# Graph attention, second layer: all row gathers issued in one run, outputs kept in gathered rows, dot products and sums alternating by tile

## The chip, the cores and the metric

The kernel runs on one core of one Trainium2 chip. The metric is device time in microseconds (us) of that core, median of three executions. One further execution was recorded by the profiler; every row below comes from it, and its times count from the start of its span.

## The reference

Two residual layers over N = 2048 nodes with D = 512 features; `adj` is a sparse 0/1 matrix with at most 8 neighbours in a row for these inputs. All is float32.

```
h = relu(layernorm(x));  x = x + GAT(h, adj)        # first layer: 16 heads, leaky relu, softmax, elu
h = relu(layernorm(x));  x = x + dense_att(h, adj)  # second layer

second layer:  q, k, v = h @ Wq.T + bq, h @ Wk.T + bk, h @ Wv.T + bv
               z = (q @ k.T) / sqrt(D) * adj;  z = where(z == 0, -10000, z)
               x + relu(softmax(z) @ v)
```

A node needs the `h` rows of its few neighbours and, for the masked entries, the sum of all rows times one small weight. A node without neighbours gets the mean of all rows.

## The kernel before

Nodes are ranked by their number of neighbours and handled in T = 16 tiles of 128 nodes. `SLOTS` says how many neighbours a tile keeps: 1, 1, 1, 1, 0, 8, 2, 5, 2, 4, 2, 3, 2, 3, 2, 3, in all 40. One gather fetches one neighbour row (512 floats) for each of the 128 nodes of a tile, so the layer has 40 gathers. GpSimd issues them (`gather1`, L1188 to L1191) as indirect DMAs out of `h1_dram`, where the first layer has stored `h` tile by tile (L1185), and counts them in `got[t]`.

The second layer, by engine. Each engine works through its own list in the order written; semaphores link the lists.

- TensorE (PE): `queries(t)` (L1275, L1278) makes u = h (Wq, Wk), most of it while the first layer still runs; the last ones of that stretch are tiles 12 and 13, tiles 14 and 15 come inside the second layer (`U1_AT`). One matmul with ones sums all rows of `h` (L1305). Then per tile k `transposes1(k)` (L1318, called T(k) here) turns the weighted sum, and `products(k)` (L1329, L1331, called P(k)) multiplies it by Wv. The order is T(k), P(k-1), but P(k-1), T(k) where k opens a part.
- VectorE (DVE): `dot(t)` (L929) waits for all slots of the tile and takes one dot product of u with each gathered row. Over a part of several tiles (`PARTS`) `scores1` (L948 to L953) masks and finds the maximum, `normalise1` (L960 to L967) makes the weights, and `aggregate1(t)` (L973) adds weight times row into `hb[t % 4]`, one instruction a slot.
- ScalarE (ACT): copies u out of PSUM (`copy_u`, L1026 and L1027), takes the exponentials of a part (`exp_scores1`, L1083, L1084), fills `hb` with the weighted sum of all rows (`base_of`, L1076), copies the transposes to SBUF (L1104) and applies the last relu (`output`, L1091) into one of four buffers `o_t`.
- GpSimd (POOL): after `gather1` of tiles 0 to 8 (21 gathers) it alternates `put(t)` (L1195), an indirect DMA that adds the tile's output to `out` in DRAM, with `gather1(9 + t)`. The residual x1 was stored to `out` in the first layer (L1177) for every tile.

The DVE list before is: wait for the sum matmul, copy it (L982), `constants`, then dots, scores and weights of tiles 0 to 3 and their sums; then for each part all its dots and scores, with the sums of the part before (the last of them between scores and weights). The ACT list before begins with `copy_u(13)` and then `exp_scores1(0)`, `base_of(0)`, `base_of(1)`. In its loop over k it waits for T(k), copies it, runs `exp_scores1` if k + 2 opens a part, then `base_of(k + 2)`, then `output(k - 1)`, which waits for P(k-1).

`row(k)` places gathered row k in buffers that the first layer has done with: 20 in `shared`, the next in `x1`, the last four in `w_out`.

Of the kernel before, what the change touches and what calls it, by code (L numbers as in the profile page):

```python
# [6 lines left out]
ALU = mybir.AluOpType  # L7
ACT = mybir.ActivationFunctionType
# [47 lines left out]
U1_AT = {4: 14, 6: 15}  # L56
# [15 lines left out]
QK_AT = (4, 7, 10)  # L72
NBAD = TOP + 1 + 2 * T + T * TOP
# [540 lines left out]
def sparse_layers(nc, v):  # L614
# [8 lines left out]
    with ctx:  # L623
# [92 lines left out]
        out_stored = [sem(f"out_stored{i}") for i in range(4)]  # L716
# [6 lines left out]
        o_t = [lone[:, 0, :], lone[:, 1, :], lone[:, 2, :], bv_bc[:, :]]  # L723
# [4 lines left out]
        PARTS = [(0, 4), (5, 2), (7, 2), (9, 3), (12, 4)]  # L728
# [4 lines left out]
        def row(k):  # L733
            if k < FLAT_ROWS:
                return shared[:, k * D:(k + 1) * D]
            if k < FLAT_ROWS + T:
                return x1[:, k - FLAT_ROWS, :]
            return w_out[:, k - FLAT_ROWS - T, :]
# [10 lines left out]
        with block:  # L749
            @block.vector  # L750
            def _(dve):
# [188 lines left out]
                def scores1(g):  # L940
                    t0, n = PARTS[g]
                    zz, qq, m = z[:, t0:t0 + n, :], zq[:, t0:t0 + n, :], zm[:, t0:t0 + n]
                    for t in range(t0, t0 + n):
                        dot(t)
                    if t0 == EARLY:
                        constants(EARLY, T)
                    dve.wait_ge(dot_done, dots[0])
                    step(dve.tensor_tensor(zz, zz, zp[:, t0:t0 + n, :], ALU.add))  # L948
                    step(dve.tensor_scalar(qq, zz, 0.0, NONE, ALU.is_equal, ALU.mult))
                    step(dve.tensor_tensor(zz, zz, qq, ALU.add))  # L950
                    step(dve.tensor_reduce(m, zz, AX_X, ALU.max))
                    step(dve.tensor_scalar(m, m, NONE, None, ALU.max))
                    dve.tensor_tensor(zz, zz, bc(zm, t0, n), ALU.subtract).then_inc(z_ready, 1)  # L953
# [26 lines left out]
                step(dve.memset(z[:, :, :], 0.0))  # L980
                dve.wait_ge(h_sum_mm, 1)
                dve.tensor_copy(h_sum, bank[0]).then_inc(sums_ready, 1)  # L982
                constants(0, EARLY)
                scores1(0)
                normalise1(0)
                for t in range(4):
                    aggregate1(t)
                for g in range(1, len(PARTS)):
                    t0, n = PARTS[g]
                    if g > 1:  # L990
                        for t in range(PARTS[g - 1][0], t0 - 1):
                            aggregate1(t)
                    scores1(g)
                    if g > 1:
                        aggregate1(t0 - 1)
                    normalise1(g)
                for t in range(*(PARTS[-1][0], T)):
                    aggregate1(t)

            @block.scalar  # L1000
            def _(act):
# [68 lines left out]
                copy_u(13)  # L1070
# [9 lines left out]
                def exp_scores1(g):  # L1080
                    t0, n = PARTS[g]
                    act.wait_ge(z_ready, g + 1)
                    act.activation(z[:, t0:t0 + n, :], z[:, t0:t0 + n, :], ACT.Exp)  # L1083
                    act.activation(e0[:, t0:t0 + n], zm[:, t0:t0 + n], ACT.Exp, bias=none[:, :], scale=-1.0).then_inc(z_exp, 1)  # L1084
                    act.wait_ge(weights_ready, g + 1)

                def output(t):
                    act.wait_ge(o_done, t + 1)
                    if t >= 4:
                        act.wait_ge(out_stored[t % 4], 16 * (t // 4))  # L1090
                    act.activation(o_t[t % 4], bank[2 + t % 4], ACT.Relu).then_inc(o_ready, 1)  # L1091

                act.wait_ge(sums_ready, 1)
# [3 lines left out]
                exp_scores1(0)  # L1097
                base_of(0)
                base_of(1)
                for k in range(T):  # L1100
# [4 lines left out]
                    if k + 2 < T:  # L1105
                        if k + 2 in first_of:
                            exp_scores1(first_of[k + 2])
                        base_of(k + 2)
                    if k >= 1:
                        output(k - 1)  # L1110
                    if k in U1_AT:
                        copy_u(U1_AT[k])
                output(T - 1)
# [10 lines left out]
            def _(pool):  # L1124
# [46 lines left out]
                for t in range(T):  # L1171
# [5 lines left out]
                    pool.indirect_dma_start(out[:, :], bass.IndirectOffsetOnAxis(own[:, t, :], 0), x1[:, t, :], None).then_inc(x1_stored, 16)  # L1177
# [15 lines left out]
                def put(t):  # L1193
                    pool.wait_ge(o_ready, t + 1)
                    pool.indirect_dma_start(out[:, :], bass.IndirectOffsetOnAxis(own[:, t, :], 0),  # L1195
                                            o_t[t % 4], None, compute_op=ALU.add).then_inc(out_stored[t % 4], 16)

                pool.wait_ge(hid_ready, T - 2)
                pool.wait_ge(x1_stored, T * 16)
# [3 lines left out]
                for t in range(9):  # L1203
                    gather1(t)
                for t in range(T):
                    put(t)
                    if 9 + t < T:
                        gather1(9 + t)
                for i in range(4):
                    pool.wait_ge(out_stored[i], T // 4 * 16)  # L1210

            @block.tensor
            def _(pe):
# [88 lines left out]
                queries(12)  # L1302
                pe.wait_ge(summed, T)
                pe.wait_ge(hidT_done, T)
                pe.matmul(bank[0], ones[:, 0:P], h_acc).then_inc(h_sum_mm, 1)  # L1305
                queries(13)
# [374 lines left out]
```

## Time and profile before

| | us |
|---|---|
| three executions | 498.70, 500.84, 495.36 |
| median | 498.7 |
| the profiled execution | 501.12 |
| its span | 499.6 |
| its mean granted TensorE clock | 0.912 of full |
| busy in the span: PE, DVE, POOL, ACT | 396.3, 371.2, 273.6, 244.4 |

The span runs from the first to the last instruction of the program; the time lies some 1.5 us above it. Busy shares are means over the whole program. The change touches the second layer alone, from about 360 us of the span on, so they say little here. The first layer's last tile is normalised at about 360 us, the last matmul of the program ends at about 481.5 us.

### The profile page before, as it was taken

To read this page: it belongs to the slowest core of one execution; us is meant where nothing else is said; L and a number is where in the kernel's file an instruction comes from. 1 tells how busy PE (TensorE), PEld (TensorE's weight loads), DVE (VectorE), ACT (ScalarE), POOL (GpSimd) and SP (SyncE) were. 2 spreads that over 40 slices of the span, in tenths; PEclk is the share of its full clock that TensorE was granted. 3 is DMA by queue.
4 is the path that set the end of the run, shared out by engine and by line. 5 is a ranking of instruction groups with operands and counts; after the bars stand their busy time and mean duration, and the time that the engine had idled before them with its cause. 6 is when DMAs were issued, how large, how long until landed. Compare 5 with 4: busy or idle time off the path is not lost.

```text
span 499.6 us, 6189 instructions
## 1 busy us (share of the span) xinstructions
PE 396.3 (79%) x2033; PEld 287.0 (57%) x2044; DVE 371.2 (74%) x715; ACT 244.4 (49%) x511; POOL 273.6 (55%) x283
## 2 busy tenths in 40 slices
PE   2899999994979888886778698889890499896950
PEld 2788888783867777852546454555680255443520
DVE  2999999977899898958679898778511478987300
ACT  1579777848888697823222344353510342342310
POOL 1344422236886776866705877774567268861330
PEclk9699999997999898999797988999997599997995
DMA  7979997300002432354413344531246347863450
GB/s 268 409 292 363 362 354 288 127 31 3 8 7 27 125 88 87 91 167 150 133 61 103 111 128 147 171 131 62 106 152 209 102 105 150 168 143 46 62 64 3
DMA packets 24290, 70.00 MB, mean 140 GB/s; under 512 B 6208, under 2 KB 6464, under 8 KB 22080
## 3 DMA queue, kind: packets, MB, share of 16 engines
q0 software_dynamic: 14336, 42.63, 31.0%
q1 hardware_dynamic: 9536, 26.96, 14.7%
q8 instruction: 17, 0.28, 0.2%
q14 instruction: 17, 0.14, 0.1%
q10 hardware_dynamic: 384, 0.00, 0.0%
HBM read 52.45 MB, written 17.12 MB: 139 GB/s over the span
## 4 chain that ended last, share of the span: by engine, by line
DVE 28%; PE 17%; POOL 15%; issue 10%; DMA 4%; ACT 1%; SPq 0%; DVEq 0%; ACTq 0%
PE psum L1331 6%; POOL record_dram L1127 4%; PE psum L1278 3%; PE psum L1234 3%; POOL s_shared L1147 3%; POOL s_shared L1165 3%; POOL s_rs L1176 2%; DVE s_shared L835 2%; DVE w_seq L929 2%; DVE s_shared L769 2%; DMA s_shared<-seq_dram,tab 2%; DVE s_shared L762 2%; DVE s_shared L760 2%; DVE s_st L853 2%; DVE s_x L851 2%
## 5 line engine op out<-in xcount | busy, mean ns | idle before, releaser
L1008 ACT ACTIVATE s_shared<-psum,seq_all 128x320 bf16<-128x320 f32 x192 | 81.6, 584 | 15.2 <-PE psum L1234 11.1
L1234 PE MATMUL psum<-s_shared 128*128 128x198 bf16 x768 | 76.4, 261 | 8.6 <-POOL s_shared L1147 8.6
L1234 PEld LDWEIGHTS psum<-s_shared 128*128 128x128 bf16 x768 | 71.5, 101 | 14.6 <-POOL s_shared L1147 10.3
L532 PE MATMUL psum<-w_seq,hT 128*128 128x272 f32 x256 | 63.2, 402 | 0.0
L1256 PE MATMUL psum<-w_out,hT 128*128 128x512 f32 x128 | 60.7, 620 | 0.9 <-ACT hT L1042 0.5
L1278 PE MATMUL psum<-w_qk,s_early 128*128 128x257 f32 x240 | 57.4, 393 | 0.0
L532 PEld LDWEIGHTS psum<-w_seq,hT 128*128 128x128 f32 x256 | 48.9, 195 | 10.0 <-issue 0.3
L1278 PEld LDWEIGHTS psum<-w_qk,s_early 128*128 128x128 f32 x240 | 46.5, 199 | 7.0
L1054 ACT ACTIVATE h_t<-s_x,s_nm,s_rs 128x512 f32<-128x512 f32 x16 | 13.0, 814 | 64.6 <-DVE s_nm L864 64.6
L1165 POOL DMA_INDIRECT s_shared<-seq_dram,tab x28 | 34.9, 1246 | 10.8 <-issue 8.2
L456 DVE MAX8 near<-adj_ring 128x8 f32<-128x2048 f32 x16 | 36.5, 2284 | 5.7 <-DMA adj_ring<-in_adj_dram 5.7
L1256 PEld LDWEIGHTS psum<-w_out,hT 128*128 128x128 f32 x128 | 25.7, 201 | 25.8 <-issue 25.0
L257 POOL TENSOR_TENSOR rstd<-veps,power 128x1 f32<-128x1 f32 x16 | 9.0, 560 | 56.8 <-DVE veps L444 56.8
L1195 POOL DMA_INDIRECT out_dram<-s_lone,tab x12 | 20.1, 1674 | 33.9 <-ACT s_lone L1091 32.4
L1147 POOL TENSOR_TENSOR s_shared<-s_shared 128x1056 f32<-128x1056 f32 x16 | 31.3, 1955 | 10.3 <-DVE s_shared L762 10.2
L459 DVE FIND_INDEX8 tab<-near,adj_ring 128x8 uint32<-128x2048 f32 x16 | 36.6, 2286 | 0.0
L1331 PE MATMUL psum<-wv_t,hT 128*128 128x512 f32 x64 | 32.9, 663 | 3.0 <-ACT hT L1104 2.9
L1176 POOL TENSOR_TENSOR s_rs<-s_ve,power 128x1 f32<-128x1 f32 x16 | 13.5, 845 | 35.0 <-DVE s_ve L857 34.9
L769 DVE TENSOR_SCALAR s_shared<-psum,neg_s 128x320 bf16<-128x320 f32 x64 | 30.7, 541 | 0.0
L356 ACT ACTIVATE squares<-adj_ring 128x2048 bf16<-128x2048 f32 x16 | 30.4, 1898 | 0.0
L1331 PE MATMUL psum<-wv_t,bout_bc 128*128 128x512 f32 x64 | 28.8, 592 | 0.1
L1026 ACT ACTIVATE seq_all<-psum 128x257 f32<-128x257 f32 x15 | 5.8, 385 | 45.4 <-PE psum L1278 26.6
(249 smaller groups left out, 783.3 us busy)
## 6 DMA issues: line engine op xcount, KB each, us to landing
adj_ring<-in_adj_dram SPq DMA_DIRECT2D x16, 1024.0 KB, 7.5
seq_dram<-seq_all POOLq DMA_DIRECT2D x16, 264.0 KB, 3.7
x_ring<-in_x_dram SPq DMA_DIRECT2D x16, 256.0 KB, 8.2
w_seq<-in_L_gnn_W_seq_dram SPq DMA_DIRECT2D x1, 1024.0 KB, 6.1
w_q<-in_L_gnn_W_q_dram SPq DMA_DIRECT2D x1, 1024.0 KB, 14.7
w_k<-in_L_gnn_W_k_dram SPq DMA_DIRECT2D x1, 1024.0 KB, 16.6
w_v<-in_L_gnn_W_v_dram SPq DMA_DIRECT2D x1, 1024.0 KB, 8.2
w_out<-in_L_gnn_W_out_dram SPq DMA_DIRECT2D x1, 1024.0 KB, 10.9
```

The costliest lines, as they stand in the source:

```text
L356: act.activation(squares[:, :], adj_ring[:, t % AR, :], ACT.Square, accum_out=square[:, t:t + 1]).then_inc(adj_squared, 1)
L456: step(dve.max(near[:, t, :], adj_ring[:, t % AR, :]))
L459: dve.max_index(record[:, t, 0:TOP], near[:, t, :], adj_ring[:, t % AR, :]).then_inc(adj_searched, 1)
L532: last = pe.matmul(bank[2 + 2 * (t % 2) + i][:, 0:SX // 2], hT[:, t % 2, c * P:(c + 1) * P], w_seq[:, c, i * (SX // 2):(i + 1) * (SX // 2) ...
L769: last = dve.tensor_scalar(ind[i][:, j, PAD:], bank[6 + i][:, 0:LN], neg_s2[:, j - SIGNS, n:n + 1], 2.0, ALU.is_gt, ALU.mult)
L1008: last = act.activation(ind[i][:, j, PAD:], bank[4 + i][:, 0:LN], ACT.Sign, bias=seq_all[:, j, D + n:D + n + 1])
L1147: pool.tensor_tensor(split[i][:, :, 2, :], split[i][:, :, 1, :], top_half(split[i][:, :, 1, :]), ALU.subtract).then_inc(r2_done, 1)
L1165: pool.indirect_dma_start(G(t)[:, s, :], None, seq_dram[:, :], bass.IndirectOffsetOnAxis(tab[:, t, s:s + 1], 0)).then_inc(got[t], 16)
L1234: last = pe.matmul(acc(i)[:, k, 0:3 * W2], ind[i][:, j, k * P:(k + 1) * P], rhs.rearrange("p t w -> p (t w)"), start=(j == 0 and k != 1), ...
L1256: last = pe.matmul(bank[2 + k % 2], hidT[:, c * P:(c + 1) * P], w_out[:, c, :], start=False, stop=(c == C - 1))
L1278: last = pe.matmul(bank[u_bank(t) + i][:, 0:hi - lo], h1T(t)[:, c * P:(c + 1) * P], w_qk[:, c, lo:hi], start=False, stop=(c == C - 1))
L1331: last = pe.matmul(bank[2 + t % 4], aT[t % 2][:, c * P:(c + 1) * P], wv_t[:, c, :], start=False, stop=(c == C - 1))
```

## The change

Five parts, all in the second layer:

1. POOL issues the gathers of all 16 tiles in one run, then the outputs. For this the 40 rows each get a place of their own: 14 tiles of `x1` rather than 16, `w_out`, and two rows of `lone`.
2. `output(t)` writes into the tile's first gathered row (`o_row`), no longer into four buffers, and no longer waits for an earlier output's DMA.
3. The last two tiles (LAST = 2) are no longer stored to `out` in the first layer (two L1177 less). At the end DVE adds relu and x1 in one instruction each, and POOL writes the tile whole, without the adding DMA.
4. DVE no longer waits for the sum matmul before its first dots; dots of later tiles stand between the sums of earlier ones; parts are four rather than five (tiles 5 to 8 are one).
5. The sum matmul goes ahead of `queries(12)`; `copy_u(13)` goes behind `base_of(1)`; `queries(14)` and `(15)` come one and two tiles earlier. In the ACT loop `output(k - 1)` now stands ahead of `base_of(k + 2)` (except at k = 2), the exponentials behind it at k = 2, 7, 10, and the wait for weights is apart.

```diff
-U1_AT = {4: 14, 6: 15}
+U1_AT = {3: 14, 4: 15}
+LAST = 2
-        PARTS = [(0, 4), (5, 2), (7, 2), (9, 3), (12, 4)]
+        PARTS = [(0, 4), (5, 4), (9, 3), (12, 4)]
+        EXP1_AT = {2: 1, 7: 2, 10: 3}
...
-            if k < FLAT_ROWS + T:
-                return x1[:, k - FLAT_ROWS, :]
-            return w_out[:, k - FLAT_ROWS - T, :]
+            k -= FLAT_ROWS
+            if k < T - LAST:
+                return x1[:, k, :]
+            k -= T - LAST
+            if k < C:
+                return w_out[:, k, :]
+            return lone[:, k - C, :]
+
+        def o_row(t):
+            if t >= T - LAST:
+                return x1[:, t, :]
+            return row(FIRST_SLOT[t]) if SLOTS[t] else lone[:, 2, :]
...
+                constants(0, EARLY)
+                for t in range(4):
+                    dot(t)
+                scores1(0)
                 dve.wait_ge(h_sum_mm, 1)
                 dve.tensor_copy(h_sum, bank[0]).then_inc(sums_ready, 1)
-                constants(0, EARLY)
-                scores1(0)
                 normalise1(0)
+                aggregate1(0); aggregate1(1); dot(5); aggregate1(2); dot(6); dot(7); dot(8)
+                scores1(1); aggregate1(3); normalise1(1)
+                dot(9); aggregate1(5); aggregate1(6); dot(10); aggregate1(7); dot(11)
+                scores1(2); aggregate1(8); normalise1(2)
+                dot(12); aggregate1(9); dot(13); dot(14); aggregate1(10); dot(15)
+                scores1(3); aggregate1(11); normalise1(3)
+                for t in range(12, T):
                     aggregate1(t)
+                for t in range(T - LAST, T):
+                    dve.wait_ge(o_done, t + 1)
+                    dve.scalar_tensor_tensor(x1[:, t, :], bank[2 + t % 4], 0.0, x1[:, t, :], ALU.max, ALU.add).then_inc(o_added, 1)
...
                 def output(t):
                     act.wait_ge(o_done, t + 1)
-                    if t >= 4:
-                        act.wait_ge(out_stored[t % 4], 16 * (t // 4))
-                    act.activation(o_t[t % 4], bank[2 + t % 4], ACT.Relu).then_inc(o_ready, 1)
+                    act.activation(o_row(t), bank[2 + t % 4], ACT.Relu).then_inc(o_ready, 1)
...
                 exp_scores1(0)
+                act.wait_ge(sums_ready, 1)
+                act.wait_ge(weights_ready, 1)
                 base_of(0)
                 base_of(1)
+                copy_u(13)
                 for k in range(T):
...
                     act.activation(aT[k % 2], bank[k % 2], ACT.Copy).then_inc(aT_done, 1)
-                    if k + 2 < T:
-                        if k + 2 in first_of:
-                            exp_scores1(first_of[k + 2])
+                    if k == 2:
                         base_of(k + 2)
-                    if k >= 1:
+                    if 1 <= k <= T - LAST:
                         output(k - 1)
+                    if k in EXP1_AT:
+                        exp_scores1(EXP1_AT[k])
+                    if k + 2 in first_of:
+                        act.wait_ge(weights_ready, first_of[k + 2] + 1)
+                    if k != 2 and k + 2 < T:
+                        base_of(k + 2)
...
+                def put_whole(t):
+                    pool.wait_ge(o_added, t - (T - LAST) + 1)
+                    pool.indirect_dma_start(out[:, :], bass.IndirectOffsetOnAxis(own[:, t, :], 0),
+                                            o_row(t), None).then_inc(out_stored, 16)
...
-                for t in range(9):
+                for t in range(T):
                     gather1(t)
-                for t in range(T):
+                for t in range(T - LAST):
                     put(t)
-                    if 9 + t < T:
-                        gather1(9 + t)
+                for t in range(T - LAST, T):
+                    put_whole(t)
...
-                queries(12)
                 pe.wait_ge(summed, T)
                 pe.wait_ge(hidT_done, T)
                 pe.matmul(bank[0], ones[:, 0:P], h_acc).then_inc(h_sum_mm, 1)
+                queries(12)
                 queries(13)
```

## Rows read from the trace of the kernel before

**Rows 1.** Busy time by stretch: start:end, length, engines, PE clock, DMA share, GB/s
```profile
376.00:388.00 12.00, 0.00 (x0) 0.00 (x0) 0.93 (x6) 0.39 (x2) 8.96 (x11) 0.69 0.67 210
...
465.00:482.00 17.00, 16.03 (x49) 7.70 (x48) 3.76 (x5) 6.01 (x11) 6.20 (x4) 1.00 0.48 63
```

**Rows 2.** Waits, 364 to 392 and 395 to 500 us: total, times, longest
```profile
ACT seq_all L1026 <- remote: 15.8, 1, 15.8
...
DVE w_seq L929 <- DMA w_out<-h_dram,tab: 1.1, 1, 1.1
```

**Rows 3.** Timeline, turn of the layers: start, us, engine, line, work
```profile
359.97 1.03 POOL L1177 DMA_INDIRECT out_dram<-s_x,tab  x1 [0.19 <-issue]
...
364.93 0.98 POOL L1190 DMA_INDIRECT s_shared<-h_dram,tab  x1 [2.55 <-DMA h_dram<-h_t,tab]
...
372.12 0.69 DVE L982 COPY w_seq<-psum 128x512 f32<-128x512 f32 x1 [10.43 <-PE psum L1305]
372.22 3.64 PE L1278 MATMUL psum<-w_qk,s_early 128*128 128x257 f32 x16
...
375.82 0.19 DVE L948 TENSOR_TENSOR hT<-hT 128x32 f32<-128x32 f32 x1
...
376.91 0.19 DVE L953 TENSOR_TENSOR hT<-hT 128x32 f32<-128x32 f32 x1
...
387.61 0.39 ACT L1026 ACTIVATE seq_all<-psum 128x257 f32<-128x257 f32 x1 [15.76 <-remote]
...
388.60 0.16 DVE L960 TENSOR_TENSOR hT<-hT,s_others 128x4 f32<-128x4 f32 x1 [11.50 <-issue]
...
389.67 1.33 ACT L1076 ACTIVATE h_t<-w_seq,hT 128x512 f32<-128x512 f32 x2 [1.10 <-issue]
...
390.50 1.42 DVE L973 SCALAR_TENSOR_TENSOR h_t<-s_shared,hT,h_t 128x512 f32<-128x512 f32 x2 [0.54 <-issue]
...
391.40 1.94 PE L1318 MATMUL psum<-ident,h_t 128*128 128x128 f32 x8 [15.54 <-issue]
```

**Rows 4.** Stretches as in rows 1, around two falls of the PE clock
```profile
395.00:401.00 6.00, 5.22 (x7) 2.42 (x9) 4.70 (x13) 2.02 (x4) 0.00 (x0) 0.50 0.00 0
...
452.50:458.50 6.00, 3.89 (x8) 2.20 (x9) 5.23 (x14) 2.57 (x6) 1.55 (x1) 0.50 0.01 2
459.50:465.00 5.50, 5.50 (x17) 2.57 (x16) 0.63 (x1) 0.60 (x1) 1.55 (x1) 1.00 0.46 53
```

**Rows 5.** Chain that ended last, second layer: start, us, what
```profile
402.42 0.22 PE psum L1329
402.63 3.43 PE psum L1331 x8
406.07 0.45 PE psum L1318 x4
...
444.46 4.29 DMA w_out<-h_dram,tab
...
449.47 0.60 DVE w_seq L929
```

**Rows 6.** Timeline and groups of the second layer: sums, gathers beside them
```profile
409.28 6.26 DVE L973 SCALAR_TENSOR_TENSOR h_t<-s_shared,hT,h_t 128x512 f32<-128x512 f32 x8 [0.56 <-DVE hT L967]
...
454.61 1.11 PE L1318 MATMUL psum<-ident,s_shared 128*128 128x128 f32 x4 [4.62 <-DVE s_shared L973]
...
L1190 POOL DMA_INDIRECT s_x<-h_dram,tab x16 | 16.9, 1058 | 4.9 <-issue 4.9
```

**Rows 7.** Last tile: timeline from 477 us; issue to landing of a plain store
```profile
481.54 0.60 ACT L1091 ACTIVATE bv_bc<-psum 128x512 f32<-128x512 f32 x1 [3.05 <-PE psum L1331]
482.42 1.55 POOL L1195 DMA_INDIRECT out_dram<-bv_bc,tab  x1 [1.92 <-ACT bv_bc L1091]
...
h_dram<-h_t,tab POOLq DMA_INDIRECT x16, 2.9
```

**Rows 8.** Gathers of the first layer: duration in ns, min, median, max
```profile
L1165 POOL DMA_INDIRECT s_shared<-seq_dram,tab x28: 945/1010/3137, 215.2 to 330.6; - x28
```

## What I expected of the change

> **What bounds the kernel now.** I read the page's header for the span, then busy time by stretch, then the waits, then the timeline around the turn of the layers, and last the chain. In [rows 1] the stretch 376 to 388 us has no PE work and almost none on DVE and ACT, while POOL goes on issuing; from 465 to 482 us PE is busy 16.0 of 17 us. So the second layer starts late, and ends on PE. [Rows 2] name the start: ACT's copy of u waits 15.8 us, without an issuer that the profile can name. DVE waits 10.4 us for the sum matmul before it does anything (372.12 in [rows 3]). For a gathered row DVE waited 1.1 us in all after 395 us. Rows that come sooner are therefore worth nothing by themselves; what can be won is what starts sooner.
>
> The timeline [rows 3] shows how the late start hangs together. The scores of tiles 0 to 3 are out at 377.1 (376.91 + 0.17). They go to ACT, whose list has `copy_u(13)` first. The matmuls for it were issued at 372.22 and should have ended near 375.9, yet the copy begins at 387.61. Only then come the exponentials, the weights (388.60 to 389.63), the bases and the first sum at 390.50. What holds that copy for 11.7 us the profile does not say; I call it the stall.
>
> **What each part costs.** Unit prices: T(k) 0.45 and P(k) 0.22 + 3.43 = 3.65 at full clock [rows 5]; a query 3.7, six score instructions 1.27, from the exponentials to the weights 1.03, a base 0.66 (two in 1.33) [rows 3]; one slot of a sum 0.78 (eight in 6.26) [rows 6]; one dot 0.6 [rows 5]; a relu or PSUM copy by ACT 0.6 [rows 7]. Semaphore hops cost 0.03 to 0.3. With these I walk through the engines' lists by hand: an instruction starts when its engine is free and its last wait is over. To see what such a walk is worth I took it through the old order too, with the old issue times of the gathers, the copy at 387.61 and half clock where [rows 4] have it: the last product ends at 483.0, where the trace has 481.5 (ACT's relu starts at 481.54 [rows 7]). Only differences of walks are used below.
>
> *First layer.* Two stores (L1177, 1.03 and a gap each) leave POOL's list. The one ahead of the last `h` store lets it, and the first gather (364.93), go 0.4 sooner: 364.5. It takes nothing else off a path.
>
> *Gathers.* The pitch is 1.26 while POOL does nothing else: 364.93 to the next. Gathers beside sums and dots take 1058 ns in the mean [rows 6], with gaps about 1.4. From issue to landing I take 4.0, between 2.9 for a store [rows 7] and 4.3 [rows 5]. Rows 3, 11, 18 and 20 then land at 372.3, 382.4, 391.2 and 393.7, row 24 at 399.3, the last one near 420. The first three bound DVE, the rest don't: the last dot comes near 445. The 14 adding stores now queue behind the gathers, until 416. They have room: 14 at some 1.9 each end near 443, and tile 13's output isn't there before 466.
>
> The Trainium skill (SBUF — State Buffer, "The DVE blocks DMA trap") says that descriptors of POOL's DMAs can't be written while DVE holds the shared port. Here the trace shows a mild form at most, 1058 ns beside DVE work [rows 6] against 945 for the quickest gather [rows 8]. By the row the sum stays; by the rule it becomes the last rival below.
>
> *The start.* DVE's dots of tiles 0 to 3 end at 372.9, scores at 374.2, then the sum's copy, which PE has ready by then since its matmul goes ahead of a query. Weights 375.9, base 376.6, sum of tile 0 at 377.5 (before: 390.50 + 0.75). PE ends `queries(13)` near 375.9, if the stall does not hold it, and T(0) is done at 378.2. So 13 us are won at the start, and most are given back next.
>
> *Tiles 1 to 5.* T(2) needs the sum of tile 2, which stands behind `dot(5)`, which waits for row 11: sum 388.1, T(2) 388.8, P(1) 392.4. T(3) needs the sum of tile 3, which stands behind dots 6 to 8 and the scores of the part 5 to 8; row 18 gives 394.3 for `dot(7)`, 395.5 for `dot(8)`, 396.8 for the scores, 397.5 for the sum. PE has stood from 382.7 to 388.3 and from 392.4 to 397.8. [Rows 4] show half clock (0.50, the 1.2 GHz level) after such idling, for some time into the work that follows: 395 to 401 after PE resumed at 391.40 [rows 3], and 452.5 to 458.5 around the resumption at 454.61, after 4.6 idle [rows 6]. I take T(3) and P(2) whole at half clock, 4.1 lost (bounds: 0, and twice that). P(2) ends at 406.0.
>
> The ACT order bites here: base 5 stands behind `output(2)`, so behind P(2). Output 406.6, base 407.3, sum of tile 5 at 413.6. PE meanwhile does query 14, T(4), P(3) (413.8), query 15, P(4): 421.1. T(5) 421.5.
>
> *Tiles 6 to 11.* Each base waits for the product of the tile three before. Base 7 stands behind T(5): 423.4, sum of tile 7 (5 slots) 427.4, PE waits 1.6. P(6) 431.7, output, exponentials, weights 433.8, base 9 434.6, sum 9 438.5, sum 10 443.1 (dots 13 and 14 stand ahead; PE waits 2.9), sum 11 449.0 (`dot(15)`, constants and the scores ahead; PE waits 1.8). P(10) 453.4, P(11) 457.0.
>
> *Tiles 12 to 15.* PE-bound with P(12) held for its copy: P(12) 461.9, then 4.1 a tile: P(15) 473.8. Against the old walk, 483.0 - 473.8 = 9.2 less.
>
> *Tail.* Before: relu, an adding store issued in 1.55 at 482.42. Now an add of 0.7 on DVE, a plain store of 1.0 that lands after 2.9. The adding store is slower to issue by 0.55, and I put another 1.1 on its landing: between 0 (no dearer) and 1.4 (the 4.3 of [rows 5] against 2.9). The add costs 0.1 more than the relu. Won: 0.55 + 1.1 - 0.1, about 1.6. What follows the landing is untouched.
>
> **Sum.** 9.2 + 1.6 = 10.8. The profiled execution would have a span of 499.6 - 10.8 = 488.8 and a time of 490.3; it lies 2.4 above the median, 498.7, from which 487.9.
>
> **Rivals.**
> - *No clock lost* (0.16). The waits at 382.7 and 392.4 are each under 6 us. The walk without the half clock ends at 469.7: 13.3 + 1.6 = 14.9, 483.8. Against it: an idle time of 4.6 before 454.6 was enough [rows 6].
> - *The stall stays on PE* (0.20). `copy_u(13)` no longer gates the exponentials, but if it is PE itself that is late until 387.6, T(0) is too, and DVE stops at the sum of tile 2 for want of base 2. With half clock to 398 the walk ends at 476.7: 6.3 + 1.6 = 7.9, 490.8. For it: the stall shows in all of [rows 1]'s engines and nothing before it is changed much. Against a larger price: in the forecast PE stands idle half of that time anyway.
> - *Half clock again* (0.16). The waits at T(7), T(10), T(11) are 1.6 to 2.9. If two of them bring a fall as at 452.5 (6 us at half in [rows 4], under 9.5 in all; I take 6.8, half of it lost), the time is 487.9 + 6.8 = 494.7, within 1%.
> - *Slower: PE is held as long as gathers run* (0.07). The stall lay inside the run of 21 gathers, POOL busy 8.96 of 12 us [rows 1]. The run now lasts until 416. If PE started T(0) at 415, the walk would end at 504.1: 504.1 - 483.0 - 1.6 = 19.5 more, 518. It decides from a start after 394. Against it: PE ran at full pace through 372.22 to 375.86 with gathers under way.
> - *Slower: gathers starve beside DVE* (0.05). One gather beside sums in the first layer took 3137 ns [rows 8]. Were each of the last 19 that long (pitch 3.4), `dot(15)` would wait for the row landing at 459, and the walk without clock loss ends at 490.0: 7.0 - 1.6 = 5.4 more, 504.1. It needs a pitch above some 2.4 us; the median there is 1010 ns and a gap of 0.3. This is what the rule of the skill named above would do.
>
> **How the numbers follow.** Forecast 0.36, the rivals as given. A measurement of this kernel can't tell less than about 1% from no change. Faster by over 1% (under 493.7) hold the forecast and the first two: 0.72. Within 1% the third: 0.16. Slower the last two: 0.12. The range runs from just under the first rival, 482, to a little over the third, 497 (P(k) and landing prices a few tenths off in 16 tiles); outside lie the slower cases, 0.12, and some 0.08 for a larger gain.
>
> **What would show it.** First sum of tile 0 near 377.5, not 390.5; DVE idle before the sum of tile 5 and before that of tile 7, released by ACT (L1076 of before); PE idle twice between 382 and 398, with a granted clock of 0.5 there or just after; gathers ending near 416; last product near 472 to 474. I am wrong if ACT's outputs ahead of bases don't hold DVE (then the gain is over 20), if T(0) starts after 387, or if PE waits for DVE behind tile 12.

## The result, and the profile after

| | before | changed |
|---|---|---|
| median, us | 497.03 (495.06 to 500.84, 4 runs) | 511.67 (509.95 to 514.02, 4 runs) |
| ratio of times | | 1.029, 95% interval 1.020 to 1.038 |
| profiled execution, its span | 501.12, 499.6 | 509.95, 508.4 |
| last product ends, from there to the end of the span | 481.5, 18.1 | 492.1, 16.3 |

A few executions came out slower as a whole; medians and ratios here and below leave them out (one each of e7 and e10, and these two are the ones that their profiles show).

The changed kernel is slower by 2.9%, where I had forecast 2% faster. The start came as expected: the first sum is at 375.1 rather than 390.5 us. Then the engines wait for each other's semaphores, although the work that is to set them is done.

Busy time by stretch of the changed kernel (columns as in [rows 1]):

```profile
376.00:388.00 12.00, 6.14 (x15) 3.07 (x16) 7.50 (x22) 1.87 (x4) 9.29 (x9) 0.60 0.65 195
388.00:400.00 12.00, 5.70 (x16) 2.37 (x15) 4.53 (x15) 0.60 (x1) 9.15 (x9) 0.93 0.71 202
400.00:415.00 15.00, 1.11 (x4) 0.71 (x4) 2.10 (x7) 1.21 (x2) 11.52 (x12) 0.50 0.71 205
415.00:430.00 15.00, 10.46 (x35) 6.52 (x36) 7.37 (x21) 4.75 (x11) 3.79 (x3) 0.74 0.46 67
```

From 400 to 415 us PE works 1.11 of 15 us, DVE 2.10, ACT 1.21: as in the empty stretch of before [rows 1], only POOL goes on. The chain of waits of 370 to 430 us puts PE's three largest gaps to "issue", that is to nothing that the profile can name:

```profile
377.25 5.84 issue
...
393.70 16.74 issue
410.44 1.11 PE psum L1354 x4
411.55 7.99 issue
```

The timeline shows what lies in them (start, us, engine, line; in brackets the idle time before it). L1354 is T(k), L1365 and L1367 are P(k), L1132 ACT's copy of a transpose, L1117 an output, L1105 a base, L956 to L961 the scores, L981 a sum, L1222 a gather, L1227 an adding store.

```profile
361.94 0.98 POOL L1222 DMA_INDIRECT s_shared<-h_dram,tab  x1 [2.53 <-DMA h_dram<-h_t,tab]
...
375.12 1.41 DVE L981 SCALAR_TENSOR_TENSOR h_t<-s_shared,hT,h_t 128x512 f32<-128x512 f32 x2 [0.60 <-issue]
376.02 1.23 PE L1354 MATMUL psum<-ident,h_t 128*128 128x128 f32 x8 [2.32 <-issue]
382.44 0.60 ACT L1132 ACTIVATE hT<-psum 128x512 f32<-128x512 f32 x1 [4.94 <-remote]
388.78 0.60 ACT L1132 ACTIVATE bout_bc<-psum 128x512 f32<-128x512 f32 x1 [5.13 <-issue]
...
389.45 0.60 PE L1354 MATMUL psum<-ident,s_shared 128*128 128x128 f32 x4
...
390.10 3.60 PE L1367 MATMUL psum<-wv_t,bout_bc 128*128 128x512 f32 x8
...
400.69 0.40 DVE L957 TENSOR_SCALAR hT<-hT 128x32 f32<-128x32 f32 x1 [0.51 <-DVE hT L956]
...
402.79 0.19 DVE L959 TENSOR_REDUCE hT<-hT 128x4 f32<-128x32 f32 x1 [1.17 <-DVE hT L958]
404.19 0.17 DVE L960 TENSOR_SCALAR hT<-hT 128x4 f32<-128x4 f32 x1 [1.21 <-DVE hT L959]
405.60 0.19 DVE L961 TENSOR_TENSOR hT<-hT 128x32 f32<-128x32 f32 x1 [1.24 <-DVE hT L960]
...
408.39 0.60 ACT L1117 ACTIVATE s_shared<-psum 128x512 f32<-128x512 f32 x1 [19.02 <-remote]
409.63 0.75 DVE L981 SCALAR_TENSOR_TENSOR s_shared<-s_shared,hT 128x512 f32<-128x512 f32 x1 [3.84 <-issue]
410.44 1.11 PE L1354 MATMUL psum<-ident,s_shared 128*128 128x128 f32 x4 [16.74 <-issue]
412.78 0.95 POOL L1222 DMA_INDIRECT s_lone<-h_dram,tab  x1 [0.30 <-issue]
...
418.89 0.60 ACT L1132 ACTIVATE hT<-psum 128x512 f32<-128x512 f32 x1 [9.29 <-issue]
419.54 0.61 PE L1365 MATMUL psum<-bias_rows,ones_b 128*128 128x512 bf16 x1 [7.99 <-issue]
```

How to read it. T(0) and T(1) end at 376.65 and 377.25, but ACT, which waits for nothing else, copies the first at 382.44 and the second at 388.78. ACT's output at 408.39 waits for P(0), over at 389.61. The trace has all 16 updates of the products' semaphore: that of P(0) comes at 408.37, 18.8 us late, and that of P(1), over at 393.70, at 419.67, 26.0 us late. T(2) is over at 390.05. Its copy stands behind that output and the base in ACT's list, and ACT, free from 409.60 on, starts it at 418.89, 28.8 us after the end of T(2). From 402 to 406 the score instructions wait 1.2 us each for the semaphore of the one ahead of them on DVE itself; before, six of them took 1.27 us together [rows 3].

So semaphore updates of PE and, later in the run, of DVE arrive late. Those of ACT do not: P(0) starts 0.06 us after the end of the copy that it waits for, P(2) 0.05 us, and the sum at 409.63 starts 0.03 us after its base. I call this late updates, and measure each as the recorded update less the end of the instruction that makes it. Some updates are missing in the trace (of T(k) in this one, 3 of 16); there I take the start of an instruction that waits for nothing else, or, where that can't be told, the last instruction that can have made the update, so that a figure is a lower bound. All late updates lie inside the run of 40 gathers (the last is issued at 412.78, its rows have landed at 416.9) and up to 7 us behind that last issue. So does the stall of before: one update of PE 11.7 us late at 387.59, in the run of 21 gathers, and one 2.2 us late behind it.

Later on nothing is late, and the kernel goes as forecast. The waits of the whole execution have one line for the bases behind the outputs (over 5 us of it ahead of the sum of tile 7), and the last two stores are the plain ones:

```profile
DVE s_shared L981 <- ACT s_shared L1105: 11.8, 4, 5.5
...
489.43 1.00 POOL L1232 DMA_INDIRECT out_dram<-s_x,tab  x1 [2.63 <-DVE s_x L1028]
```

### The profile page after: what moved, and what is told of

Its sections match the earlier page's. It is cut to its first block, busy times and chain, and to the rows that moved or that the text cites. A ratio compares the mean times of both kernels' runs of the same rounds, so it can differ in the third digit from the quotient of the medians.

```text
span 508.4 us, 6167 instructions
## 1 busy us (share of the span) xinstructions
PE 399.8 (79%) x2044; PEld 288.3 (57%) x2044; DVE 369.0 (73%) x703; ACT 243.8 (48%) x507; POOL 268.8 (53%) x281
## 4 chain that ended last, share of the span: by engine, by line
PE 26%; DVE 21%; POOL 12%; issue 12%; ACT 2%; DMA 2%; SPq 0%; ACTq 0%; DVEq 0%
PE psum L1367 9%; PE psum L1314 6%; PE psum L1292 4%; PE psum L1270 3%; POOL s_shared L1178 3%; POOL record_dram L1158 2%; POOL s_shared L1196 2%; POOL s_early L1167 2%; POOL s_rs L1207 1%; DVE s_shared L772 1%; DVE s_shared L770 1%; DVE s_shared L779 1%; DVE s_shared L981 1%; PE psum L1354 1%; DVE s_shared L845 1%
## 5 line engine op out<-in xcount | busy, mean ns | idle before, releaser
L1292 PE MATMUL psum<-w_out,hT 128*128 128x512 f32 x128 | 62.5, 634 | 0.0
L1314 PE MATMUL psum<-w_qk,s_early 128*128 128x257 f32 x240 | 59.0, 401 | 0.0
L1314 PEld LDWEIGHTS psum<-w_qk,s_early 128*128 128x128 f32 x240 | 47.7, 204 | 7.4
L1367 PE MATMUL psum<-wv_t,hT 128*128 128x512 f32 x64 | 32.7, 659 | 0.0
L1367 PE MATMUL psum<-wv_t,bout_bc 128*128 128x512 f32 x64 | 28.8, 592 | 0.0
L1227 POOL DMA_INDIRECT out_dram<-s_shared,tab x8 | 12.8, 1604 | 27.2 <-ACT s_shared L1117 26.9
L1222 POOL DMA_INDIRECT s_shared<-h_dram,tab x20 | 20.2, 1011 | 8.3 <-issue 5.8
## 6 DMA issues: line engine op xcount, KB each, us to landing
w_k<-in_L_gnn_W_k_dram SPq DMA_DIRECT2D x1, 1024.0 KB, 16.4
```

What stands on the lines that cost most here:

```text
L1292: last = pe.matmul(bank[2 + k % 2], hidT[:, c * P:(c + 1) * P], w_out[:, c, :], start=False, stop=(c == C - 1))
L1314: last = pe.matmul(bank[u_bank(t) + i][:, 0:hi - lo], h1T(t)[:, c * P:(c + 1) * P], w_qk[:, c, lo:hi], start=False, stop=(c == C - 1))
L1367: last = pe.matmul(bank[2 + t % 4], aT[t % 2][:, c * P:(c + 1) * P], wv_t[:, c, :], start=False, stop=(c == C - 1))
```

## The experiments

The first theory was that a long unbroken run of POOL's indirect gathers holds back the other engines' semaphore updates. Its rival was that the new lists of ACT and DVE (outputs ahead of bases, sums between dots) make the engines wait for each other.

Late is the longest late update between 355 and 445 us, by the measure given above. The last column is the time from the first gather to the end of the last product, which takes out the few us by which the first layer differs between profiles. e4, e9, e13, e14 and e16 gather wrong or too few rows, and each was run once.

| kernel | median us (runs) | ratio to before, 95% | late, us | span of layer 2 |
|---|---|---|---|---|
| before | 497 | 1 | 11.7 | 116.6 |
| changed | 511.67 (4) | 1.029, 1.020 to 1.038 | 28.8 | 130.1 |
| e1 before, gathers in one run | 517.25 (4) | 1.039, 1.033 to 1.045 | 16.4 | 133.6 |
| e2 changed, old POOL order | 487.47 (4) | 0.980, 0.975 to 0.985 | 13.8 | 106.7 |
| e3 changed, spaced | 492.22 (8) | 0.990, 0.987 to 0.993 | none | 112.1 |
| e4 changed, half rows | 508.83 (1) | | 30.6 | 129.9 |
| e5 before, spaced | 492.69 (5) | 0.991, 0.986 to 0.996 | none | 109.3 |
| e6 e3, bases first | 491.33 (4) | 0.988, 0.984 to 0.992 | none | 110.8 |
| e7 e2, bases first | 490.74 (4) | 0.989, 0.983 to 0.994 | 6.0 | |
| e8 e2, spaced | 492.41 (6) | 0.991, 0.988 to 0.995 | none | 112.2 |
| e9 changed, half the partitions | 510.09 (1) | | 34.1 | 131.5 |
| e10 changed, small memset | 503.97 (3) | 1.015, 1.007 to 1.023 | 25.3 | |
| e11 changed, run in pieces | 489.69 (10) | 0.988, 0.985 to 0.992 | 2.6 | 111.6 |
| e12 e2, small memset | 486.86 (4) | 0.982, 0.977 to 0.987 | 14.5 | 107.4 |
| e13 changed, plain loads by POOL | 475.49 (1) | | none | 98.1 |
| e14 changed, plain loads by SP | 475.20 (1) | | none | 98.3 |
| e15 e2, one break | 491.39 (4) | 0.987, 0.981 to 0.993 | 2.8 | 112.3 |
| e16 e13, spaced | 476.17 (1) | | none | 98.4 |

### The run of gathers, put into the kernel before and taken out of the changed one

```diff
# e1, in the kernel before
-                for t in range(9):
-                    gather1(t)
                 for t in range(T):
-                    put(t)
-                    if 9 + t < T:
-                        gather1(9 + t)
+                    gather1(t)
+                for t in range(T):
+                    put(t)
# e2, in the changed kernel
-                for t in range(T):
+                for t in range(9):
                     gather1(t)
                 for t in range(T - LAST):
                     put(t)
+                    if 9 + t < T:
+                        gather1(9 + t)
```

> The kernel before with one edit: all 40 gathers of the second layer in one run, then the 16 outputs. Theory A (a long unbroken run of gathers holds back the semaphore updates of the other engines: in the changed kernel's trace a product that ended near 393.7 was seen by ScalarE at 408.4, and VectorE's own chain of steps went at 1.2 to 1.4 us a step from 400 to 407): slower than before by 8 to 25 us, 505 to 522, with gaps until the gathers end near 416. Theory B (the new lists of ScalarE and VectorE cost the time, outputs ahead of bases): no change or a few us faster, 490 to 500.

> The changed kernel with the old order on GpSimd: 21 gathers, then output t and the gathers of tile 9 + t in turn; all else as changed. Theory A: the long gap from 394 to 419 goes, a stall of some 10 us stays inside the first 21 gathers; faster than the changed kernel by 12 to 25 us, 487 to 499. Theory B: stays at 508 to 515.

The one run alone makes the kernel before 3.9% slower, with all of its old lists: PE's first update 10.9 us late, that of P(0) 16.4 us, that of P(1) 6.2 us, and gaps of the same kind as in the changed kernel. From the timeline of e1, T(0) and a step of the scores:

```profile
390.33 1.94 PE L1316 MATMUL psum<-ident,h_t 128*128 128x128 f32 x8 [14.65 <-issue]
...
418.80 0.17 DVE L949 TENSOR_SCALAR hT<-hT 128x16 f32<-128x16 f32 x1 [0.53 <-DVE hT L948]
```

Taken back in the changed kernel (e2), it is worth 511.67 - 487.47 = 24 us, and what is left of the change beats the kernel before by 2.0%. The rival can't explain either: the lists are the old ones in e1 and the new ones in e2. Updates of PE are still late in e2, in the run of the first 21 gathers: by 3.9 us for the copy of u, by 6.7 us for T(0). T(1), over at 378.19, is copied at 392.00, 13.8 us later, although ACT waits for nothing else:

```profile
392.00 0.60 ACT L1132 ACTIVATE bout_bc<-psum 128x512 f32<-128x512 f32 x1 [6.51 <-issue]
```

### The same run, spaced out

```diff
# e3, in gather1 of the changed kernel; pause is [P, 256] floats
+                        if paused_no[0]:
+                            pool.wait_ge(paused, paused_no[0])
+                        pool.memset(pause[:, :], 0.0).then_inc(paused, 1)
+                        paused_no[0] += 1
                         pool.indirect_dma_start(row(FIRST_SLOT[t] + s), ...)
```

e5 does the same to the first 21 gathers of the kernel before, e8 to the first 21 of e2.

> The changed kernel with a small memset of some 0.35 us ahead of each gather of the second layer, so that they go out at about 1.65 us instead of 1.26; still one run of 40. Theory A1 (the rate matters, a backlog builds up at 1.26 and not at 1.65): no late semaphore updates, 485 to 495. Theory A2 (the length of the run matters, whatever its rate): the gap lasts until the last gather near 428, 520 or more. Theory B: 510 to 520.

> The kernel before with a memset ahead of each of the first 21 gathers of the second layer (those up to tile 8, pitch about 1.45 us), nothing else. Theory A (the late semaphore update at 387.6 in the kernel before is the same effect): ScalarE's copy of u comes by 378, the first sum by 380, the time falls by 5 to 12 us to 485 to 492. Rival (the stall in the kernel before has another cause, or costs nothing): 495 to 499.

> The changed kernel with the old order on GpSimd and the first 21 gathers paced by memsets. Theory A: the late updates that the old order still has (up to 6 us at 384) go, TensorE starts the first products at once; but rows 12 to 20 land up to 4 us later and hold VectorE. 483 to 489. If the remaining late updates cost nothing, the later rows alone decide: 489 to 492.

With some 1.54 us between gathers in the mean, rather than 1.30 (most follow at 1.26), no update is late in any of the three. In e3 ACT copies T(0) at once (379.13, where the changed kernel took 5.8 us), the score steps start some 0.2 to 0.3 us apart, and the idle times of PE have names and come near those that I had forecast (5.6 and 5.4 us):

```profile
378.46 1.23 PE L1361 MATMUL psum<-ident,h_t 128*128 128x128 f32 x8 [1.95 <-DVE h_t L982]
379.13 0.60 ACT L1133 ACTIVATE hT<-psum 128x512 f32<-128x512 f32 x1 [0.52 <-PE psum L1361]
...
390.79 1.11 PE L1361 MATMUL psum<-ident,s_shared 128*128 128x128 f32 x4 [7.19 <-DVE s_shared L982]
...
402.96 1.11 PE L1361 MATMUL psum<-ident,s_shared 128*128 128x128 f32 x4 [6.15 <-DVE s_shared L982]
```

e5 shows that the stall of before was the same thing: spaced, the old kernel gains 0.9%, its update of 11.7 us is on time and the first sum comes at 377.8. Its time, 492.69, lies just above the 485 to 492 that I had expected. e8 shows the price of spacing: rows come later. It is 5 us slower than e2, although e2 has the late updates (492.41, just above the 489 to 492 expected for that case).

### The order of bases and outputs

```diff
# e6 in e3, e7 in e2: ACT's loop
-                    if 1 <= k <= T - LAST:
+                    if k == 2:
                         output(k - 1)
...
                     if k != 2 and k + 2 < T:
                         base_of(k + 2)
+                    if k != 2 and 1 <= k <= T - LAST:
+                        output(k - 1)
```

> The changed kernel with paced gathers (as the paced run, 492.2) and ScalarE's bases put back ahead of the outputs, except at k = 2. If the output ahead of the base holds VectorE as much as the prediction made of it, 5 us or more less: under 487. By a walk through the lists the two orders differ by 1.3 us only: 490 to 492. If the order does not matter: 492.

> The changed kernel with the old order on GpSimd (487.5) and the bases ahead of the outputs. Walk: 1 to 2 us less, 485.5 to 487. If bases ahead of outputs delay the outputs and with them the gathers that stand behind an output on GpSimd: 488 to 491.

With nothing late, the order is worth 112.1 - 110.8 = 1.3 us of the second layer between one profile each; the times, 492.22 and 491.33, have intervals that overlap, so that this is not clear of noise. On the old POOL order it costs some 3 us instead. A likely reason, which no run shows by itself, is that outputs come later, and so do the gathers that stand behind their stores: in its profile the last one comes 78.3 us after the first, against 72.0 in e2. The rival falls: the order that I had blamed in advance for DVE's waits does cause them, but it isn't where 24 us went.

### What about the run: bytes, rows, pitch, length?

```diff
# e4: source and destination cut to half rows; h1_half views h1_dram as rows of 256
-   pool.indirect_dma_start(row(FIRST_SLOT[t] + s), None, h1_dram[:, :], ...)
+   pool.indirect_dma_start(row(FIRST_SLOT[t] + s)[:, 0:D // 2], None, h1_half, ...)
# e9: 64 of the 128 partitions
+   pool.indirect_dma_start(row(FIRST_SLOT[t] + s)[0:P // 2, :], None, h1_dram[:, :], ... tab[0:P // 2, t, s:s + 1] ...)
# e10: as e3, the memset one column wide; e12: the same for the first 21 gathers of e2
# e11: the changed kernel, its run in pieces of 12, 9, 9, 7 and 3
                 for t in range(T):
                     gather1(t)
+                    if t in (5, 8, 11, 14):
+                        pool.wait_ge(got[t], 32 * SLOTS[t])
# e15: as e11, but in e2 and behind t == 5 alone
```

> The changed kernel with each gathered row cut to 256 of its 512 floats (wrong rows, the other half stays what the buffer held), as many gathers, descriptors and semaphore updates as before at half the bytes. If it is the bytes that hold back the updates, the gap goes and the time is under 498; if it is the gathers as such (issue, descriptors, updates of semaphores), the gap stays and the time is 505 to 515.

> The changed kernel with every gather of the second layer for 64 of the 128 partitions only (half the tile is not gathered): half the rows to fetch in each gather, as many gathers and as many semaphore updates a gather. If the updates of the gathers' semaphores crowd out those of the engines, the gap stays as long or grows (gathers may go out faster): over 505. If it is the number of rows (descriptors and packets) a us, no late updates: under 492.

> The changed kernel with a memset of one column ahead of each gather, pitch about 1.38 us between the 1.26 that backs up and the 1.5 that does not. If the limit lies under 1.38: no late updates and rows sooner than in the paced run, 488 to 491. If above: late updates of a few us, 495 to 508.

> The changed kernel, gathers at full rate, with GpSimd waiting for the landing of all gathers so far behind tiles 5, 8, 11 and 14 (runs of 12, 9, 9, 7 and 3, breaks of some 3 us). If late updates are a backlog that builds up over about ten gathers and drains in a break: few late updates, 486 to 492. If a break does not drain it: 500 or more.

> The changed kernel with the old order on GpSimd and a memset of one column ahead of each of the first 21 gathers. If 1.38 us is slow enough: no late updates and rows only 2 to 3 us later, 484 to 488. If not: as the old order alone, 487 to 489.

> The changed lists with the old order of gathers and stores, and one wait of POOL for the landing of row 11 (after the gathers of tile 5), some 3 us. With a backlog that builds over some ten gathers and drains in a break, the two late updates of the version without the break (3.9 us and 6.1 us late) become under 2 us, while rows 12 to 20 come 3 us later; I expect a gain of 0 to 2 us over that version, that is 485 to 488. If the number of gathers since the start of the run does not matter, the updates stay late and the time is 488 to 491.

Half the bytes don't take the late updates away, and neither do half the rows, which made the pitch a little shorter still: the issue of a gather took 0.90 to 0.92 us for 64 rows and 0.96 for 128. In e4 T(2) is copied 30.6 us after its end, in e9 T(1) 34.1 us. First a line of e4, then, from the timeline of e9:

```profile
409.16 1.12 PE L1355 MATMUL psum<-ident,s_shared 128*128 128x128 f32 x4 [18.48 <-issue]
```

```profile
384.49 0.90 POOL L1222 DMA_INDIRECT s_shared<-h_dram,tab  x1 [0.30 <-issue]
...
397.59 0.61 PE L1365 MATMUL psum<-bias_rows,ones_b 128*128 128x512 bf16 x1 [23.57 <-issue]
```

The small memset of e10 was to space the gathers by a little; it went into the gap of 0.30 us that was there, and most gathers still followed at 1.26. The late updates stayed too (25.3 us at worst), and POOL's own memsets signalled up to 2.65 us late. So what helps in e3 is the spacing and not the memset as such. In e11 the rate within a piece is the full one, but POOL stops for about 3 us at the end of each, until its rows are in:

```profile
375.20 0.95 POOL L1222 DMA_INDIRECT s_shared<-h_dram,tab  x1 [0.30 <-issue]
379.24 1.28 POOL L1222 DMA_INDIRECT s_shared<-h_dram,tab  x1 [3.09 <-DMA s_shared<-h_dram,tab]
```

The updates late by 1.8 to 2.6 us come in before the first break is over, and none is late behind it, and the time is 22 us under that of the changed kernel. So something builds up by about the tenth gather and is gone after 3 us of rest. My expectation for e15 was missed: one break brought the worst update from 13.8 down to 2.8 us late, more than the 2 us that I had allowed, and the time rose by 4 us. Rows 12 to 20 come 3 us later, and PE now idles 6.0 and 6.7 us, each with a half clock around its end (6.8 us at 0.50 twice), where e2 idled 6.8, 1.3 and 1.7 with one half clock of 10.2 us. The late updates of e2 lie where PE has little to do anyway. e12 says the same from the other side: an update 14.5 us late, and a time equal to that of e2.

### Indirect, or any run of loads?

```diff
# e13: plain loads from fixed rows, issued by POOL
-                        pool.indirect_dma_start(row(FIRST_SLOT[t] + s), None, h1_dram[:, :], ...).then_inc(got[t], 16)
+                        b = (FIRST_SLOT[t] + s) % T
+                        pool.dma_start(row(FIRST_SLOT[t] + s), h1_dram[b * P:(b + 1) * P, :]).then_inc(got[t], 16)
# e14: the same loads issued by SP, started by a semaphore that POOL sets; DVE waits on semaphores of
# their own, and SP on earlier dots from tile 10 on, since these semaphores are used twice
# e16: e13 with a memset of 384 columns ahead of each load
```

> The changed kernel with its 40 indirect gathers replaced by 40 plain loads issued by POOL on the same queue: same sizes (128 rows of 2 KB), same semaphores, fixed source rows, so the neighbours that enter the second layer are the wrong ones; nothing else is left out. If what holds the other engines back is any long run of DMAs issued by POOL, the semaphore updates of PE stay late by over 5 us and the time stays above 500. If it is the indirect form (POOL reading the indices and writing the descriptors for them), no update is late by more than 2 us and the time falls to 492 or less (the walk of the prediction with gathers at full rate gives 488).

> The same 40 plain loads, but issued by SP on its own hardware queue, on semaphores of their own (16 updates each, as before), with the adding stores still on POOL; wrong neighbours as in the kernel with POOL's plain loads. POOL then does nothing between the last store of the first layer and the first output. If the late updates come from the DMA traffic or from its 16 semaphore updates a transfer, whoever issues it, they stay late by over 5 us and the time stays above 500, provided the loads land at a rate near one in 1.3 us. If they come from POOL's issuing, none is late by more than 1 us, and the time is 484 to 489.

> POOL's 40 plain loads again (wrong neighbours, nothing else left out), but with a memset ahead of each, so that one goes out every 1.2 to 1.3 us and the run lasts about as long as that of the 40 indirect gathers, 50 us. If the indirect form is the cause, no semaphore update of PE, DVE or ACT is late by over 1 us, and the time is 484 to 492, as the prediction's walk has it with rows at that pace. If it is a long run at this pace in any form, PE's updates are late by over 5 us from some ten loads on, and the time is above 500.

No update is late in any of them. e13 issues its 40 loads in 20.7 us rather than 50.8 and moves bytes nearly twice as fast as the gathers did; timeline, then the busy time by stretch:

```profile
359.75 10.76 POOL L1223 DMA_DIRECT2D s_shared<-h_dram  x20 [2.33 <-DMA h_dram<-h_t,tab]
```

```profile
364.00:376.00 12.00, 10.56 (x47) 7.82 (x48) 10.57 (x40) 4.54 (x11) 12.00 (x24) 1.00 0.99 370
376.00:388.00 12.00, 8.24 (x23) 3.99 (x22) 11.62 (x45) 3.94 (x8) 8.42 (x12) 0.86 1.03 386
```

At 370 to 386 GB/s, against 205 in the changed kernel, with as many transfers of the same size and 16 semaphore updates each, nothing is held back. So it is neither the traffic nor the number of semaphore updates, nor POOL's queue as such. e16 rules out most of the other reading, that e13's run is over too soon: its 40 loads last from 359.8 to 395.1, at a pitch of 0.88 us (I had meant 1.26), far beyond the 15 us after which the changed kernel's updates were late. What is left is the indirect form, when one follows the other at 1.26 us. These kernels read fixed rows in a block where the gathers read scattered ones; no run has an indirect gather of rows in a block, so the issue and the scattered source are not told apart. All three times lie well under what I had expected (484 and more for e14 and e16). The likely reason is that the rows come so much sooner: PE's longest idle time in the second layer of e13 is 3.2 us, where e3 has 7.2 and 6.2.

## Why the prediction was wrong

**The start** held. First sum at 375.1 (forecast 377.5), T(0) over at 376.7 (378.2), queries(13) over at 373.7 (375.9). Part of this is the first layer, which ended sooner in this execution: the first gather came at 361.9 (forecast 364.5), 2.6 us early.

**The stall** is the step that failed, and with it the price of a semaphore hop. I wrote that the matmuls of `queries(13)` "should have ended near 375.9", that the profile does not say what holds the copy, and then priced the change as if the stall went with `copy_u(13)`, every later hop at 0.03 to 0.3 us. The stall didn't belong to that copy but to the run of gathers around it: the trace of before shows it in hardly more than one instruction, because few that wait for PE ran there. The change did two things to it. It made the run 40 long rather than 21, and it moved into it the work of tiles 0 to 3, with a semaphore hop between engines at each step. There hops from PE took 3.1 to 28.8 us. e1 shows the longer run alone (3.9% slower), e5 the effect in before (0.9%).

**Tiles 1 to 5.** T(3) was forecast for 397.8 and came at 410.4, 12.6 later, because the update of P(0) reached ACT at 408.4 and base 3 stood behind it; the score steps, with 7 us on DVE rather than 1.3, were over just before. P(2) was forecast to end at 406.0 and ended at 424.9: another 6.3, from the copy of T(2), which came at 418.9. Those 18.9 us stay: the last product ends at 492.1, and the walk has 473.8, or 472.3 less the 1.5 by which it ran above the trace of before. The span came out 508.4 - 488.8 = 19.6 above its forecast. Counted from the first gather, 2.6 us more are missing each time, 21.5 at P(2); the median lies 511.67 - 487.9 = 23.8 above the forecast.

**Everything else in the sum** was about right, and e3 is the test of it. Its T(3) starts at 402.96, 5.2 after the forecast, as its spacing has it: row 18, which the sum of tile 3 waits for, goes out 18 pitches behind the first, each some 0.28 us longer. Its last product ended at 476.9, forecast 473.8. The run of gathers in the changed kernel lasted 51.8 us (forecast 51.5). DVE waited for bases 5 and 7, released by ACT. PE idled twice near where I had it (7.2 and 6.2 us in e3, each with a half clock of 6.8 us around its end). The tail was shorter by 18.1 - 16.3 = 1.8 us (forecast 1.6). The time of e2, 487.5, is near my 487.9 by chance: it has other rows, other waits and fewer gathers in its run.

**The rivals.** "PE is held as long as gathers run" had a chance of 0.07 and was the nearest to what happened, but as a mechanism it was off: PE was not held. It started T(0) at 376.0, far under the 394 from which that rival was to decide, and ran whatever it was told of. What was held was the news of finished work, PE's above all. My argument against it, that PE ran at full pace from 372.22 to 375.86 with gathers under way, excluded only a held engine: those 3.6 us of matmuls wait for nobody. I should have asked for an instruction that receives an update in the run, and the one that I had there, the copy of u, was 11.7 us late. Its price, 518, was nearer than the forecast. "The stall stays on PE" (0.20) kept the old stall at its old length, and so came out faster than before. "Gathers starve beside DVE" did not occur: the longest gather of the run took 1.43 us and the mean pitch was 1.30. The rule of the Trainium skill (SBUF — State Buffer, "The DVE blocks DMA trap"), which that rival stood for, speaks of DVE instructions in a 2-port mode. No run shows whether these dots and sums are such; beside them the trace shows no more than those 1.43 us. The range, 482 to 497, was too narrow for the same reason: it had late updates in no term.

## What to carry to other kernels

An idle time that the profile puts to "issue" or "remote", with the awaited work long over, is a cost of its own; find out what else ran then (here a row of back-to-back indirect gathers) before pricing a change that lengthens it or moves work into it. Keep such runs short, some ten, with other work or a wait of 3 us between, or space them at 1.5 us; but weigh what later rows cost, since the fastest version that gathers the right rows (e2, 2.0% faster than before; e12 equals it) keeps 21 in a row and tolerates late updates where PE has little to do. Where rows can be laid out so that a plain load fetches them, it is worth much more: e13, e14 and e16, with the wrong rows, took 475 to 476 us in one execution each.

## What the runs showed of the hardware

- Back-to-back indirect gathers from POOL at a pitch of 1.26 us (mean 1.30) delay the semaphore updates of PE, by up to 28.8 us in the changed kernel. In e2 an update 7.1 us into the run is on time, and the next one of PE, 11.8 us into it, about at the tenth gather, is 3.9 us late; in the changed kernel the first late one is 3.1 us late. DVE's updates are on time there up to 393.0; of those behind some are late, by 1.2 to 3.5 us, while T(3) starts 0.06 us after its sum. POOL's memsets in e10 signalled up to 2.65 us late. No update of ACT was found late. The last late ones come 4.1 to 7.6 us after the last gather of a run of 40 is issued.
- At a pitch of 1.54 us in the mean none is late; in runs of 12, 9, 9, 7 and 3 with 3 us between, 2.6 us at most. The gathers themselves stay on time in the changed kernel: most take 0.96 us to issue, and their rows have landed 3.0 to 4.3 us after it, from the first to the last.
- It doesn't go away with half the bytes (e4) or half the rows for each gather (e9), and plain loads of the same size don't do it, from POOL or SP, at 0.53 or 0.88 us pitch and up to 386 GB/s.
- Late updates come in a rhythm: those of the changed kernel between 399.96 and 408.37 are 0.70 or 1.40 us apart, and so are those of e1 near 420 (418.78, 419.48, 420.18, 420.89). That looks like one update let through at a time, each 0.70 us, but no run tested it. What in the indirect form holds them, and why ACT's go free, stays open.
